# Weights of attention loaded and split by quarters inside the attention block, with scores and column sums moved around the fourth projection

## The chip, the cores and the metric

The kernel runs on one core of a Trainium2 chip. The metric is the device time of one execution in microseconds (us), and the time before is the median of three runs. A profiled execution gives the trace. TensorE is called PE there, VectorE DVE, ScalarE ACT, GpSimd POOL and SyncE SP; SPq, ACTq and PEq are the engines' sequencers, and SPq's DMA_DIRECT2D is the issue of a transfer.

## The reference, cut to what matters

Three layers follow one another, each with a residual and a LayerNorm: causal attention (scores are multiplied with a lower triangular mask, not set to minus infinity, before the softmax), a routed layer that picks one of four contexts by token, and a gated feed-forward layer with 2:4 sparsity. The change lies in the attention and in what comes ahead of it.

```python
B, T, D, HEADS = 4, 512, 512, 16
q = (x @ Wq).reshape(B, T, H, Dh); k = (x @ Wk)...; v = (x @ Wv)...
scores = jnp.einsum('bthd,bshd->bhts', q, k) * tril
attn = softmax(scores / T ** 0.5)
out = jnp.einsum('bhts,bshd->bthd', attn, v).reshape(B, T, H * Dh) @ Wo
x = layernorm(x + out)
```

## The kernel before

All of it is computed in float32 accuracy with halves: each operand is a high part (`hi`, rounded by a ScalarE copy to float32r) and a low part (`lo`, the raw value minus the high one, on VectorE), and a product is three matmuls per block of 128 rows of the contraction (hi hi, hi lo, lo hi; `matmul3`, lines 31 to 43). With D = 512 there are KT = 4 such blocks, so a product of 128 x 512 is 12 matmuls.

`prepare` (lines 1066 to 1102) is a block of its own ahead of attention. SyncE issues one load of 1 MB for each of wq, wk, wv and wo and one for x_t of batch 0 (x transposed). ScalarE copies each whole matrix to its high half and VectorE subtracts for the low half; GpSimd builds the identity that transposes need. All engines meet at the block's end, and only then does `attention` (line 46) begin.

Attention's block has a program for each engine, ordered by hand and tied by semaphores. Ahead of the loop for batch 0, ScalarE and VectorE split x_t by quarters (lines 542 and 676). TensorE then alternates for g = 0 to 3 between `project(0, g)` (even g is a q, odd g a k projection; g // 2 = m names the group of four heads; line 366) and `v_product(g)` (line 421), with the routing's counts behind g = 1. Projections all go to one PSUM bank, `PJ`. `split_proj` cuts q and k to halves (ScalarE line 517, VectorE line 640). `v_split` cuts v in three: high (ScalarE, line 547), the rest (VectorE, line 684), its bf16 half (ScalarE, line 550) and what then remains (VectorE, line 689, for batch 0; GpSimd's `v_last`, line 264, for the other batches). VectorE also makes the routing's indices in pieces between the v blocks (`route.chain`, lines 931 to 990).

SyncE's `stack_up(b, g)` (line 319) writes both halves of a projection to DRAM (lines 324 and 326), waits until they are there, and loads them again with another layout, in four transfers of 256 KB (line 332). These stacks (`big_lo` in the rows) are what the scores read. The stack g = 0 and 1 serves heads 0 to 3 (m = 0), g = 2 and 3 the next four. `G_AHEAD` is 4: four projections are made ahead of the loop.

Behind the v products come `v_sum(0, 0..2)` (nine matmuls, line 434), the column sums of v for the parts of the sequence above the diagonal; VectorE adds them up in `v_above` (lines 697 and 700). Then come the scores of units 0 to 2 (line 390), then the loop `batch(0)`. A unit is one of 48 per batch: one head and one or two blocks of rows, so that 12 units share a stack (UPM = 12). Step u of the loop does the transposes of unit u (line 401), the scores of unit u + 3, a piece of a later projection, and the values of unit u - 2 (line 417). VectorE's maxima (line 651) run two units ahead, ScalarE's exponentials (line 528) one ahead of `hi` (line 538). At u = 0 TensorE waits for all three column sums, since banks 5 and 6 hold them. SyncE loads x_t of the next batch behind the first four stacks (line 340). GpSimd adds up the parts of each head (`sum_parts`, lines 204 to 207) once ScalarE has copied them out.

## Time and profile before

| what | value |
|---|---|
| time, median of 3 runs | 1152.39 us (1150.78 to 1152.79) |
| the profiled execution | 1151.63 us, span 1149.8 us |
| TensorE busy | 1047.3 us, 91% of the span |
| VectorE, ScalarE, GpSimd busy | 751.2, 479.7, 281.9 us |
| attention of the four batches | about 22 to 465 us of the span |
| routed layer and feed-forward | from about 465 us on |

How to read it: the span is the time from the first to the last instruction of the one execution that was traced, and the shares of busy time are means over stages that have different limits. A row of the timeline names the start and duration in us, the engine, the line of the kernel, the operation, what it writes and reads, and in brackets the engine's idle time before it with what ended it. A row of the windows gives a stretch, its length, the busy time of each engine with its instructions, TensorE's mean granted clock, the busy share of the DMA engines and what they moved.

### The profile page before, as it was taken

Reading aid. Unit: us, or ns where it says so; the run is one execution under the profiler, and the core shown is the slowest. Engines: PE = TensorE matmul, PEld = TensorE weight load, DVE = VectorE, ACT = ScalarE, POOL = GpSimd, SP = SyncE. Lnnn points to the kernel's source line nnn. Section 1 sums busy time; section 2 is a strip of 40 time slices with the busy share of each in tenths; the row PEclk is TensorE's granted clock in tenths of the full one; section 3 lists DMA queues with packets and bytes.
Section 4 is the critical chain, followed back from the end, with each engine's and each line's share of the span. In section 5 each row is a group of like instructions: output and inputs, shape, how many; then the busy total and the mean of one; then the engine's idle time right before and its main releaser. Section 6 shows DMA issues by size and latency. Waiting matters only on the chain.

```text
span 1149.8 us, 18016 instructions
## 1 busy us (share of the span) xinstructions
PE 1047.3 (91%) x6022; PEld 846.0 (74%) x6023; DVE 751.2 (65%) x1764; ACT 479.7 (42%) x882; POOL 281.9 (25%) x482
## 2 busy tenths in 40 slices
PE   2898998998899976699999999999999999999994
PEld 1576766776676765488788888888888888888873
DVE  4689778868876886356664845665565545664666
ACT  4278658846864894122333322221231222222113
POOL 1036545723744462022220002300000000000222
PEclk9999999999999998799999999999999999999997
DMA  5776726735671670122444102310010101100001
GB/s 184 195 190 180 196 93 166 202 93 169 180 191 49 158 248 19 64 80 78 157 154 166 37 1 24 51 37 1 1 56 17 36 0 36 37 1 1 38 37 73
DMA packets 54016, 106.18 MB, mean 92 GB/s; under 512 B 6064, under 2 KB 6064, under 8 KB 53936
## 3 DMA queue, kind: packets, MB, share of 16 engines
q1 hardware_dynamic: 49056, 90.99, 28.5%
q0 software_dynamic: 4880, 14.18, 3.3%
q8 instruction: 44, 0.72, 0.3%
q14 instruction: 36, 0.29, 0.1%
HBM read 72.11 MB, written 30.94 MB: 90 GB/s over the span
## 4 chain that ended last, share of the span: by engine, by line
PE 56%; DVE 2%; ACT 0%; issue 0%; DMA 0%; POOLq 0%; POOL 0%; ACTq 0%; DVEq 0%
PE f_bank L42 54%; PE f_bank L1396 1%; PE f_bank L1404 1%; PE f_bank L1446 1%; DVE rows_kept L1743 0%; DVE ln_stats L810 0%; DMA rows<-sorted_dram 0%; DVE hs_lo L1731 0%; DVE xt_lo L1626 0%; DVE ln_mv L812 0%; ACT L823 0%; POOLq L1190 0%; ACT xt_hi L1512 0%; DVE h L1721 0%; ACT hs_hi L1573 0%
## 5 line engine op out<-in xcount | busy, mean ns | idle before, releaser
L1682 DVE TENSOR_TENSOR h<-f_bank,fsg 128x512 f32<-128x512 f32 x64 | 44.2, 691 | 181.6 <-PE f_bank L42 181.4
L1550 ACT ACTIVATE fsg<-f_bank 128x512 f32<-128x512 f32 x64 | 38.3, 599 | 293.8 <-PE f_bank L42 293.6
L401 PE MATMUL bank<-ident,probs 128*128 128x128 f32 x640 | 109.4, 286 | 33.5 <-DVE pt_lo L671 18.7
L528 ACT ACTIVATE probs<-bank,nmax 128x384 f32<-128x384 f32 (+3 forms) x256 | 129.8, 539 | 17.8 <-DVE nmax L662 16.3
L651 DVE CUSTOM_DVE_ANT_0 bank<-bank,mask 128x384 f32<-128x384 f32 (+3 forms) x256 | 123.1, 503 | 21.1 <-PE bank L390 20.8
L671 DVE TENSOR_TENSOR pt_lo<-bank,pt_hi 128x512 f16<-128x512 f32 (+1 forms) x192 | 114.7, 597 | 16.0 <-ACT pt_hi L538 15.8
L841 POOL TENSOR_SCALAR ln_var<-ln_mv 128x1 f32<-128x1 f32 x43 | 10.0, 233 | 466.7 <-DVE ln_mv L812 466.7
L42 PE MATMUL bank<-x_hi,w_qk 128*128 128x512 f32 x256 | 103.5, 412 | 22.8 <-DVE x_lo L676 22.4
L538 ACT ACTIVATE pt_hi<-bank 128x512 f16<-128x512 f32 (+1 forms) x192 | 103.0, 536 | 33.3 <-PE bank L401 32.6
L42 PE MATMUL f_bank<-wd_hi,hs_hi 128*128 128x512 f32 x256 | 100.4, 392 | 3.2 <-DVE rows_kept L1743 3.2
L401 PEld LDWEIGHTS bank<-ident,probs 128*128 128x128 f32 x640 | 67.2, 141 | 45.0 <-ACT probs L528 23.7
L42 PE MATMUL f_bank<-wd_hi,hs_lo 128*128 128x512 f32 x256 | 100.2, 391 | 0.0
L42 PE MATMUL f_bank<-wd_lo,hs_hi 128*128 128x512 f32 x256 | 100.1, 391 | 0.0
L42 PE MATMUL f_bank<-big_hi,wg_hi 128*128 128x512 f32 x240 | 93.8, 391 | 0.0
L42 PE MATMUL f_bank<-big_hi,wu_lo 128*128 128x512 f32 x240 | 93.5, 389 | 0.0
L42 PE MATMUL f_bank<-big_hi,wg_lo 128*128 128x512 f32 x240 | 93.4, 389 | 0.0
L42 PE MATMUL f_bank<-big_lo,wg_hi 128*128 128x512 f32 x240 | 93.4, 389 | 0.0
L42 PE MATMUL f_bank<-big_hi,wu_hi 128*128 128x512 f32 x240 | 93.4, 389 | 0.0
L42 PE MATMUL f_bank<-big_lo,wu_hi 128*128 128x512 f32 x240 | 93.4, 389 | 0.0
L390 PE MATMUL bank<-big_lo 128*128 128x384 f32 (+3 forms) x256 | 83.7, 373 | 0.0
L417 PEld LDWEIGHTS bank<-v,pt_hi 128*128 128x128 f16 x640 | 49.4, 97 | 39.0 <-issue 28.8
L417 PE MATMUL bank<-v,pt_hi 128*128 128x97 bf16 x640 | 74.7, 210 | 2.1 <-DVE pt_lo L671 1.9
(230 smaller groups left out, 2446.4 us busy)
## 6 DMA issues: line engine op xcount, KB each, us to landing
big_lo<-q_hi_dram SPq DMA_DIRECT2D x32, 256.0 KB, 4.4
big_lo<-q_lo_dram SPq DMA_DIRECT2D x32, 256.0 KB, 4.9
big_lo<-k_hi_dram SPq DMA_DIRECT2D x32, 256.0 KB, 3.7
big_lo<-k_lo_dram SPq DMA_DIRECT2D x32, 256.0 KB, 5.3
rows<-sorted_dram SPq DMA_DIRECT2D x19, 256.0 KB, 2.7
x_raw<-x_t SPq DMA_DIRECT2D x4, 1024.0 KB, 6.6
q_hi_dram<-q_hi SPq DMA_DIRECT2D x16, 256.0 KB, 2.5
q_lo_dram<-q_lo SPq DMA_DIRECT2D x16, 256.0 KB, 2.4
```

Of the source, the lines that this page charges most:

```text
L42: ins = pe.matmul(out, a(k, i), b(k, j), start=(n == 0), stop=(n == len(chain) - 1))
L390: ins = pe.matmul(S[u % SR][:, at:at + cols(r)], stack[0][m % 2][:, h, r * P:(r + 1) * P], stack[1][m % 2][:, h, 0:cols(r)], start=True, s ...
L401: ins = pe.transpose(TP[u % TR][:, j * P:(j + 1) * P], probs[u % RP][:, j * P:(j + 1) * P], ident[:, :])
L417: ins = pe.matmul(out[:, at:ONE + 1], p, v3[:, j, c, at:ONE + 1], start=(n == 0), stop=(n == len(chain) - 1))
L528: ins = act.activation(probs[u % RP][:, at:at + cols(r)], S[u % SR][:, at:at + cols(r)], ACT.Exp, bias=nmax[:, r, c:c + 1])
L538: act.activation(pt_hi[u % RP][:, 0:n], TP[u % TR][:, 0:n], ACT.Copy).then_inc(s_hi, 1)
L651: dve.tensor_tensor_reduce(out=S[u % SR][:, at:at + cols(r)], in0=S[u % SR][:, at:at + cols(r)], in1=mask[:, T - cols(r):T], scale=1.0, sc ...
L671: dve.tensor_tensor(pt_lo[u % RP][:, 0:n], TP[u % TR][:, 0:n], pt_hi[u % RP][:, 0:n], ALU.subtract).then_inc(s_lo, 1)
L1396: ins = pe.transpose(XB[q % 2][:, k * P:(k + 1) * P], rows[q][:, k * P:(k + 1) * P], ident[:, :])
L1404: ins = pe.transpose(EG[i][:, k * P:(k + 1) * P], gu[i][:, k * P:(k + 1) * P], ident[:, :])
L1550: act.activation(fsg[v % 2][:, :], GB[v % 2][:, :], ACT.Silu).then_inc(s_sg, 1)
L1682: dve.tensor_tensor(h[r % 2][:, j, :], UB[v % 2][:, :], fsg[v % 2][:, :], ALU.mult).then_inc(s_h, 1)
```

## The change

The block `prepare` is gone, and its work moves into the engine programs of `attention`. No buffers of their own hold the raw weights any more: wq lands in `probs`, wk in `v_tail` and one `v_rest`, wv in `o_raw`, wo in `z`, all of them idle at that time. SyncE issues 16 transfers of 256 KB for the weights and 4 for x_t, in the order x and wq in turn, wk, wv, the tokens, wo. ScalarE and VectorE split by quarters; the first wait is for each x and wq pair, those of the other matrices are for all four quarters. wo's low halves are subtracted by GpSimd, which also takes over the last part of v for batch 0; its clearing of `z[0]` moves behind them.

TensorE's order becomes: the projections g = 0 and 1, each block as its halves come in; the four v products; the projection g = 2; the scores of units 0 to 2; the projection g = 3; the column sums; the loop. g = 1 and 2 go to bank 4 instead of `PJ`. The cuts of g = 3 and `v_above` move into step u = 0 of the loop on ScalarE and VectorE, and TensorE waits for one column sum at u = 0 and for all of them at u = 2. The diff, cut to its core:

```diff
@@ -104,6 +104,17 @@
...
+        w_raw = [[probs[k][:, :] for k in range(KT)],
+                 [v_tail[:, k, :] for k in range(KT - 1)] + [v_rest[1][:, :]],
+                 [o_raw[:, k, :, :].rearrange("p h d -> p (h d)") for k in range(KT)],
+                 [z[k][:, :] for k in range(KT)]]
+        s_first = [sem(f"s_first{k}") for k in range(KT)]
+        s_w = [sem(f"s_w{i}") for i in range(1, len(w_dram))]
+        s_wh, s_wl = sem("s_wh"), sem("s_wl")
+        s_woh, s_wol = sem("s_woh"), sem("s_wol")
+        s_id = sem("s_id")
...
@@ -173,6 +184,10 @@
...
+        def proj_bank(b, g):
+            return bank[4] if b == 0 and g in (1, 2) else PJ
...
@@ -251,6 +266,7 @@
...
         X_HEAD = 7
+        NCONST = 6 + NB
...
@@ -266,7 +282,10 @@
...
             pool.sem_inc(s_os[1], PRIMED)
-            pool.memset(z[0][:, :], 0.0).then_inc(s_const, 1)
+            pool.memset(ident[:, :], 0.0).then_inc(s_id, 1)
+            pool.wait_ge(s_id, 1)
+            pool.affine_select(out=ident[:, :], in_=ident[:, :], compare_op=ALU.not_equal, fill=1.0, base=0,
+                               pattern=[[-1, P]], channel_multiplier=1).then_inc(s_id, 1)
...
@@ -275,10 +294,22 @@
...
                 pool.memset(n_up[:, r, :], float((NB - 1 - r) * P)).then_inc(s_const, 1)
-            pool.wait_ge(s_const, 5 + NB)
+            pool.wait_ge(s_const, 4 + NB)
...
+            for j in range(NB // 2):
+                v_last(0, j)
+            for k in range(KT):
+                pool.wait_ge(s_woh, k + 1)
+                pool.tensor_tensor(wl[3][:, k, :], w_raw[3][k], wh[3][:, k, :].bitcast(F32),
+                                   ALU.subtract).then_inc(s_wol, 1)
+            for j in range(NB // 2, NB):
+                v_last(0, j)
+            pool.wait_ge(s_wol, KT)
+            pool.memset(z[0][:, :], 0.0).then_inc(s_const, 1)
+            pool.wait_ge(s_const, NCONST)
...
@@ -312,8 +343,6 @@
...
-        NCONST = 6 + NB
...
@@ -354,7 +383,15 @@
...
+            for k in range(KT):
+                sp.dma_start(x_turned[:, k, :], x_t[0][:, k, :]).then_inc(s_first[k], 16)
+                sp.dma_start(w_raw[0][k], w_dram[0][:, k, :]).then_inc(s_first[k], 16)
+            for i in range(1, len(w_dram) - 1):
+                for k in range(KT):
+                    sp.dma_start(w_raw[i][k], w_dram[i][:, k, :]).then_inc(s_w[i - 1], 16)
             route.load(sp)
+            for k in range(KT):
+                sp.dma_start(w_raw[-1][k], w_dram[-1][:, k, :]).then_inc(s_w[-1], 16)
...
@@ -365,14 +402,18 @@
...
                 m, side = g // 2 % NM, g % 2
-                if first == 0:
-                    pe.wait_ge(s_pjl, b * 2 * NM + g)
-                if g < 2 * NM:
+                if first == 0 and (b > 0 or g > 1):
+                    pe.wait_ge(s_pjl, b * 2 * NM + g - (b == 0 and g == G_AHEAD - 1))
+                if b == 0 and g < 2:
+                    pe.wait_ge(s_xl, last // 3)
+                    pe.wait_ge(s_wl, g * KT + last // 3)
+                elif g < 2 * NM:
...
                     pe.wait_ge(s_xl, (b + 1) * KT + (last + 2) // 3)
-                ins = matmul3(pe, PJ[:, :], lambda k, i: (wh, wl)[i][side][:, k, m * P:(m + 1) * P],
+                ins = matmul3(pe, proj_bank(b, g)[:, :], lambda k, i: (wh, wl)[i][side][:, k, m * P:(m + 1) * P],
...
@@ -418,15 +459,22 @@
...
-            def v_product(j):
-                matmul3(pe, VB[j][:, :], lambda k, i: x_hl[i][:, k, j * P:(j + 1) * P],
-                        lambda k, i: (wh, wl)[i][2][:, k, :], KT).then_inc(s_vp, 1)
+            def v_product(j, fresh=False):
+                for first in range(0, 3 * KT, 3):
+                    if fresh:
+                        pe.wait_ge(s_wl, 2 * KT + first // 3 + 1)
+                    ins = matmul3(pe, VB[j][:, :], lambda k, i: x_hl[i][:, k, j * P:(j + 1) * P],
+                                  lambda k, i: (wh, wl)[i][2][:, k, :], KT, first, first + 3)
+                ins.then_inc(s_vp, 1)
...
                     pe.wait_ge(s_v2, (b + 1) * NB)
+                    if b == 0:
+                        pe.wait_ge(s_const, NCONST - 1)
...
@@ -453,6 +501,9 @@
...
                 pe.wait_ge(s_otl, b * NB + r + 1)
+                if b == 0 and r == 0:
+                    pe.wait_ge(s_wol, KT)
...
@@ -463,7 +514,10 @@
...
-                        pe.wait_ge(s_sfe, (b + 1) * (NB - 1))
+                        pe.wait_ge(s_sfe, (b + 1) * (NB - 1) if b > 0 else 1)
+                    if u == 2 and b == 0:
+                        pe.wait_ge(s_sfe, NB - 1)
...
@@ -494,16 +548,22 @@
...
-            for g in range(G_AHEAD):
-                project(0, g, 0, 3 * KT)
-                v_product(g)
-                if g == 1:
-                    pe.wait_ge(s_const, NCONST)
+            for g in range(2):
+                for first in range(0, 3 * KT, 3):
+                    project(0, g, first, first + 3)
+            for j in range(NB):
+                v_product(j, j == 0)
+                if j == 1:
+                    pe.wait_ge(s_const, NCONST - 1)
                     route.count(pe, ones_bf[:, :], counts[0], counts[1])
+            project(0, 2, 0, 3 * KT)
+            pe.wait_ge(s_vr, AHEAD_S)
+            for u in range(AHEAD_S):
+                scores(0, u)
+            project(0, 3, 0, 3 * KT)
...
                 v_sum(0, n)
-            for u in range(AHEAD_S):
-                scores(0, u)
+            pe.wait_ge(s_id, 2)
...
@@ -514,7 +574,7 @@
...
                 act.wait_ge(s_dw, b * 2 * NM * 32 + max(g - 1, 0) * 32)
-                act.activation(qk_hl[side][0][:, :], PJ[:, :], ACT.Copy,
+                act.activation(qk_hl[side][0][:, :], proj_bank(b, g)[:, :], ACT.Copy,
...
@@ -538,7 +598,10 @@
...
             def x_split(b, k):
-                act.wait_ge(s_xraw, (b + 1) * 16)
+                if b == 0:
+                    act.wait_ge(s_first[k], 32)
+                else:
+                    act.wait_ge(s_xraw, b * 16)
...
@@ -584,6 +647,8 @@
...
                         exps(b, u)
+                    if b == 0 and u == 0:
+                        split_proj(0, G_AHEAD - 1)
...
@@ -622,11 +687,25 @@
...
+            def weight_hi(i, k, done):
+                if i > 0:
+                    act.wait_ge(s_w[i - 1], KT * 16)
+                act.activation(wh[i][:, k, :], w_raw[i][k], ACT.Copy).then_inc(done, 1)
...
                 x_split(0, k)
-            for g in range(G_AHEAD):
-                split_proj(0, g)
-                v_split(0, (g,))
+                weight_hi(0, k, s_wh)
+            for i in (1, 2):
+                for k in range(KT):
+                    weight_hi(i, k, s_wh)
+                split_proj(0, i - 1)
+            for j in range(NB):
+                v_split(0, (j,))
+                if j == 0:
+                    for k in range(KT):
+                        weight_hi(3, k, s_woh)
+            split_proj(0, 2)
...
@@ -637,7 +716,7 @@
...
                 dve.wait_ge(s_pjh, b * 2 * NM + g + 1)
-                dve.scalar_tensor_tensor(out=qk_hl[side][1][:, :], in0=PJ[:, :],
+                dve.scalar_tensor_tensor(out=qk_hl[side][1][:, :], in0=proj_bank(b, g)[:, :],
...
@@ -684,10 +763,6 @@
...
                                       ALU.subtract).then_inc(s_vr, 1)
-                for j in blocks if b == 0 else ():
-                    dve.wait_ge(s_v1, b * NB + j + 1)
-                    dve.tensor_tensor(v3[:, j, :, V2:V2 + HD], v_rest[j % 2][:, :].rearrange("p (h d) -> p h d", d=HD),
-                                      v3[:, j, :, V1:V1 + HD], ALU.subtract).then_inc(s_v2, 1)
...
@@ -737,6 +812,10 @@
...
                         split_proj(b, split_at[u])
+                    if b == 0 and u == 0:
+                        split_proj(0, G_AHEAD - 1)
+                        for n in range(NB - 1):
+                            v_above(0, n)
...
@@ -763,18 +842,27 @@
...
+            def weight_lo(i, k):
+                dve.wait_ge(s_wh, i * KT + k + 1)
+                dve.tensor_tensor(wl[i][:, k, :], w_raw[i][k], wh[i][:, k, :].bitcast(F32),
+                                  ALU.subtract).then_inc(s_wl, 1)
...
                 x_split(0, k)
+                weight_lo(0, k)
+            for i in (1, 2):
+                for k in range(KT):
+                    weight_lo(i, k)
+                split_proj(0, i - 1)
             routing = route.chain(dve, counts[0], counts[1])
-            for g in range(G_AHEAD):
-                split_proj(0, g)
-                v_split(0, (g,))
+            for j in range(NB):
+                v_split(0, (j,))
...
-            dve.wait_ge(s_const, NCONST)
-            for n in range(NB - 1):
-                v_above(0, n)
+            split_proj(0, 2)
+            dve.wait_ge(s_const, NCONST - 1)
...
@@ prepare, lines 1066 to 1102 @@
-def prepare(nc, w_dram, w_split, ident, x_src, x_turned, s_xraw, D):
...
```

## Rows read from the trace of the kernel before

**Rows 1.** Busy us by stage: length, PE, PEld, DVE, ACT, POOL, clock, DMA, GB/s.

```profile
0.00:18.80 18.80, 0.00 (x0) 0.01 (x1) 9.17 (x4) 8.92 (x5) 0.68 (x6) 1.00 0.76 279
...
22.40:27.10 4.70, 4.67 (x13) 3.77 (x14) 0.00 (x0) 0.00 (x0) 0.03 (x1) 1.00 0.00 0
...
27.10:47.40 20.30, 19.88 (x87) 15.52 (x85) 12.15 (x41) 6.08 (x10) 0.00 (x0) 1.00 0.69 182
```

**Rows 2.** Timeline of the start: SyncE's last load, ScalarE's splits of wq, wk, wv.

```profile
3.20 2.32 SPq L1083 DMA_DIRECT2D x_raw<-x_t  x1
...
6.22 1.91 ACT L1096 ACTIVATE w_qk<-w_raw 128x2048 fp32r<-128x2048 f32 x1 [4.13 <-DMA w_raw<-wq]
...
9.12 1.91 ACT L1096 ACTIVATE w_qk<-w_raw 128x2048 fp32r<-128x2048 f32 x1 [0.99 <-DMA w_raw<-wk]
...
11.82 1.91 ACT L1096 ACTIVATE big_hi<-w_raw 128x2048 fp32r<-128x2048 f32 x1 [0.79 <-DMA w_raw<-wv]
```

**Rows 3.** DMA issues of the first 8 us: the load of x_t, KB, us to landing.

```profile
x_raw<-x_t SPq DMA_DIRECT2D x1, 1024.0 KB, 14.0
```

**Rows 4.** The timeline from the column sums into the loop, TensorE and VectorE.

```profile
50.19 3.73 PE L434 MATMUL bank<-v,ones_bf 128*128 128x512 bf16 x9 [2.81 <-DVE v L689]
...
53.55 0.99 PE L390 MATMUL bank<-big_lo 128*128 128x384 f32 x4
...
56.64 0.88 PE L401 MATMUL bank<-ident,probs 128*128 128x128 f32 x4 [2.09 <-ACT probs L528]
...
58.14 0.57 DVE L651 CUSTOM_DVE_ANT_0 bank<-bank,mask 128x384 f32<-128x384 f32 x1 [0.88 <-PE bank L390]
...
71.05 0.48 PE L390 MATMUL bank<-big_lo 128*128 128x384 f32 x2
```

**Rows 5.** The busy time of a stretch in batch 0's loop, in columns as above.

```profile
90.00:100.00 10.00, 7.38 (x85) 5.99 (x82) 9.93 (x40) 10.00 (x25) 5.74 (x10) 1.00 0.83 210
```

**Rows 6.** SyncE's timeline, and the landing of all stack loads from 28 to 60 us.

```profile
39.74 0.43 SPq L332 DMA_DIRECT2D big_lo<-k_lo_dram  x1
...
40.94 0.34 SPq L326 DMA_DIRECT2D q_lo_dram<-q_lo  x1
...
46.93 0.32 SPq L332 DMA_DIRECT2D big_lo<-q_hi_dram  x1
...
55.22 0.79 SPq L332 DMA_DIRECT2D big_lo<-k_hi_dram  x2
...
57.08 0.40 SPq L340 DMA_DIRECT2D x_raw<-x_t  x1
...
66.90 0.34 SPq L324 DMA_DIRECT2D q_hi_dram<-q_hi  x1
...
DMA to landing us min/median/max: 3.0/4.6/5.7
```

**Rows 7.** The timeline's splits of x_t by quarters on ScalarE and VectorE.

```profile
19.03 2.19 ACT L542 ACTIVATE x_hi<-x_raw 128x512 fp32r<-128x512 f32 x4 [2.60 <-PEq L1072]
...
19.69 2.59 DVE L676 TENSOR_TENSOR x_lo<-x_raw,x_hi 128x512 fp32r<-128x512 f32 x4 [0.94 <-ACT x_hi L542]
```

**Rows 8.** The chain that ended last: one product of 12 matmuls in the routed layer.

```profile
498.59 2.80 PE f_bank L42 x12
```

**Rows 9.** The timeline: VectorE's one-hots ahead of the counts, and a cut of k.

```profile
32.62 0.17 DVE L946 CAST tok_f<-tok_sb 128x16 f32<-128x16 int32 x1
...
32.75 0.60 ACT L517 ACTIVATE k_hi<-bank 128x512 fp32r<-128x512 f32 x1 [0.78 <-PE bank L42]
...
35.25 0.69 DVE L640 SCALAR_TENSOR_TENSOR k_lo<-bank,k_hi 128x512 fp32r<-128x512 f32 x1
```

**Rows 10.** Two lines of GpSimd: duration ns min/median/max, first and last start.

```profile
L264 POOL TENSOR_TENSOR v<-v_rest,v x12: 1122/1138/1150, 138.8 to 352.2; 128x512 bf16<-128x512 f32 x12
...
L259 POOL TENSOR_TENSOR x_lo<-x_raw,x_hi x12: 1269/1284/1302, 94.6 to 306.1; 128x512 fp32r<-128x512 f32 x12
```

**Rows 11.** TensorE's stretches of 1 us: length, busy us, granted clock, DMA share, GB/s.

```profile
51.00:52.00 1.00, 1.00 (x4) 0.50 1.04 203
```

More of the change, by code:

```diff
@@ L43, in matmul3, with attention @@
     return ins
-def attention(nc, w_split, stacks, ident, idx_all, x_t, x_raw, s_xraw, x_rows,
+def attention(nc, w_dram, w_split, stacks, ident, idx_all, x_t, x_raw, s_xraw, x_rows,
               sorted_rows, route, context, scratch, B, T, D):
@@ L1855, in build @@
             x_raw = actx.enter_context(nc.sbuf_tensor("x_raw", [P, KT * T], F32))
-            x_turned = x_raw[:, :].rearrange("p (k t) -> p k t", k=KT)
             w_vo = big[0][:, 0:4 * KT * D].rearrange("p (i k n) -> p i k n", i=4, k=KT)
@@ L1859, in build @@
             x_t = x_t.rearrange("b (k p) t -> b p k t", p=P)
-            prepare(nc, [w.rearrange("(k p) n -> p k n", p=P) for w in (wq, wk, wv, wo)], w_split, ident,
-                    x_t[0], x_turned, s_xraw, D)
-            attention(nc, w_split, big[1], ident, idx_all, x_t, x_raw, s_xraw,
+            w_dram = [w.rearrange("(k p) n -> p k n", p=P) for w in (wq, wk, wv, wo)]
+            attention(nc, w_dram, w_split, big[1], ident, idx_all, x_t, x_raw, s_xraw,
                       x.rearrange("b (r p) d -> b p r d", p=P), sorted_rows,
```

30 lines of the change are left out of this document (removed).

## The prediction, made before the changed kernel ran

> **What bounds the kernel now.** I read the busy time by stage first. Up to 18.8 us TensorE does nothing: the weights are loaded and split whole [rows 1]. It then works from 22.4 us on, 19.88 of the 20.3 us from 27.1 to 47.4 [rows 1], and has gaps again before the loop of batch 0 [rows 4]. Next comes the order of events at the start. The five loads of 1 MB are issued by 5.5 us [rows 2] and land one after the other: ScalarE waits for wq until 6.2 us, for wk until 9.1, for wv until 11.8 [rows 2], and x_t lands 14.0 us after its issue at 3.2 [rows 2, 3], so at 17.2. One more MB takes some 2.7 us. x_t, which everything needs, comes last, and attention starts only behind wo's splits. That head of about 22.4 us lies wholly on the path: nothing after it is tied to absolute time. The loop starts with the transposes at 56.64 us; VectorE takes up its work on unit 3 at 58.14 us [rows 4]. In the loop VectorE and ScalarE are all but full (9.93 and 10.00 of 10 us) [rows 5]. So whoever brings the loop's start forward by n us gains n us, whatever the 91% of TensorE on the page say, as long as the loop finds its stacks and buffers in time. The task is to compute the new start.
>
> **New loads.** The order becomes x and wq in pairs of quarters, then wk, wv, the tokens, wo. The bytes and the rows of 2 KB (512 floats) are the same, so I keep 2.7 us per MB and the landing times of the sequence in which the matrices arrived: the first pair (0.5 MB) at 4.8 us, the next ones 1.4 us apart (6.2, 7.6, 9.1), wk at 11.8, wv at 14.5, wo at 17.2 [rows 2, 3]. SyncE issues 21 transfers at 0.43 us each (the issue at 39.74) [rows 6] and a little between them, say 0.47, and is through at about 10.5 us, before it has anything else to do.
>
> **Splits.** A quarter costs ScalarE about 0.56 us (2.19 us for four) and VectorE 0.65 (2.6 us for four) [rows 7]; whole matrices cost 1.91 us on ScalarE [rows 2], so cutting costs some 0.3 us a matrix, hidden behind the loads. Pair 3 lands at 9.1; its x and w highs are done at 10.25, its lows at 11.05. TensorE starts at about 6.6 us and ends the first q projection at 11.7 to 12.3. Although wk comes in quarters, its splits wait for all four: ScalarE 11.8 to 14.05, VectorE to 15.0, TensorE's k projection to 15.7, fed by quarters. ScalarE cuts q only behind wk's highs (14.7), VectorE q's low at 15.7. wv: highs 14.7 to 16.9, k's high at 17.5, wv's lows to 18.4, k's low 19.1. The first v product ends at 19.1.
>
> **TensorE's path from there.** A product of 12 matmuls is 2.8 us at full rate [rows 8], 4.7 in the cold start [rows 1]. v product 1 ends at 21.9. Then the counts wait for the one-hots, which VectorE makes behind the first v cut: 20.5 plus 2.6 us (32.62 to 35.22 before) [rows 9] is 23.1, a stall of 1.2 us. v products 2 and 3 end at 29.1, the projection of g=2 at 31.9. The other costs here are nil, by their covers: wo's highs (2.2 us of ScalarE between the cuts of v blocks 0 and 1) lie beside the v products, and delay v's cut 1 by 1.4 us, which is made good by block 2; without that cover they would cost 2.2. wo's lows and the last v halves go to GpSimd: 4 x 1.28 + 4 x 1.14 = 9.7 us [rows 10]. Two v halves are done at 25.8, wo's lows at 31.0, the other two at 33.3 us, and the column sums want them only after the fourth projection, at about 37.4. Queued behind these on GpSimd are the clearing of z[0] and the first sums of parts, which come only some 9 us into the loop. VectorE is rid of four subtractions of 0.69 us.
>
> **The stacks, SyncE's chain.** This is what I take to be last. q's high and low writes are issued at 14.7 and 15.8 us, but queue behind wo, which lands at 17.2; before, the writes issued at 40.94 behind a stack's loads were seen done at 46.93, about 1.6 us after these loads had landed (39.74 + 5.7) [rows 6]. So q's loads start at 18.8. From the first load of a q stack to the first load of the k stack it was 46.93 to 55.22, 8.3 us, with k's halves ready, as they are here: 27.1. The last of four loads is issued three issues of 0.43 us later and lands within 3.0 to 5.7 us [rows 6]: 31.4 to 34.1; nothing queues behind it here, and I take 33.6. So the first scores start at 33.6, against TensorE free at 31.9: moving the scores ahead of projection 3 makes the stack's wait show, but also covers the projection's own stack.
>
> **From the scores to the loop.** Scores 1.0 us, projection 3 2.8 us (37.4), its high on ScalarE 0.6 and low on VectorE 0.7 behind the first maxima (38.8), v_above(0) 0.7 like the low [rows 4, 9]: the transposes start at 39.5. TensorE's three column sums (2.1 us warm; 3.73 in the row) [rows 4] run beside this. VectorE's sums 1 and 2 follow and unit 3's maxima come at 41.0, where they came at 58.14. Gain: 56.64 - 39.5 = 17.1 by the one, 17.1 by the other. Two corrections by the clock. Before the scores TensorE idles 1.7 us. After an idle of 2.8 us, and again after 2.1 us, the trace has some 3 us at a granted clock of 0.5, i.e. 1.2 GHz [rows 4, 11]; the column sums took 1.6 us more than at full rate. I charge 1.7 us (bounds 0 and 3.4, the second if the counts' stall does it too). In return the new loop starts with TensorE just busy for 6 us, where the old one lost its first 3 to 4 us at 0.5 clock; VectorE was idle 0.9 of them, as far as I see it from its rows; I credit 0.9 (bounds 0 and 1.5). Sum: 17.1 - 1.7 + 0.9 = 16.3 us. The profiled execution took 1151.63 us (span 1149.8), which gives 1135.3; the median before is 1152.39, 0.8 above it, and gives 1136.
>
> **After the loop has started.** Stack g=2 is loaded from 35.2 us (1.6 behind the k stack's landing), g=3 8.3 later, from 43.5, landed at about 50: 10.5 us into the loop. It is wanted at unit 12, issued 14.4 us into the loop (71.05 to 56.64) [rows 4]: 4 us of slack. The x_t load of batch 1 follows and lands near 54; before, it came at 0.4 us into the loop [rows 6], now at 6. g=4's writes, ready some 10 us into the loop (66.90) [rows 6], queue behind it: q's loads at 16 us into the loop, k's at 24, landed at 30.5, wanted at unit 24, which I put at twice unit 12's time and a little, 31 to 33. That costs nothing, but with 1 to 2 us of slack; if the cover is gone, TensorE waits there for as long as it is short.
>
> **A rule that speaks against it.** The Trainium skill, "DMA: Bandwidth & Descriptors", section "Bandwidth", says to batch a DMA to 1 MiB or more, since at 64 KB it measured 138 GB/s and at 1 MB 341. An estimate half way between (240 GB/s) would move the 5.2 MB in 21.8 us instead of about 14, and would take 8 us off the gain. Against that, no row of this trace has 256 KB loads of whole rows into 128 partitions queued back to back; rival C has the price by rows.
>
> **The rivals.**
> A, the forecast: the k stack ends last, gain 14.5 to 18: 1134.4 to 1137.9. Chance 0.54.
> B: the stack is in time and TensorE's path is the last: scores at 31.9, and no idle before them, so no cold stretch. Gain 17.1 + 1.7 + 0.9 = 19.7: 1132.7. For it: the loads landed in as little as 3.0 us. Against: 8.3 us per stack. Chance 0.13.
> C: the loads or the clock are worse. Quarters at the pace of the stack loads (1 MB within 1.3 + 5.7 us of the first issue, less some 1.7 us until data move, makes 200 GB/s) put wo's end at about 28 instead of 17.2 us and leave a gain of 5 to 6 (1146 to 1147); chance 0.05. Two cold stretches instead of one, a TensorE that stays at 1.2 GHz while it is fed by quarters, or a stack that comes late at unit 12 or 24, cost 1.7 to 4 us more, gain 12 to 14.5: 1138 to 1140; chance 0.21. If it never reached full rate, eight products at 4.7 to 5.1 us put the loop at about 53, still faster.
> D, slower: the transfers of one queue don't overlap, so that each quarter costs its issue to landing. wv is then through after 16 quarters. Break-even is where 17 us are lost, i.e. wv at 31.5: 1.9 us a quarter. At 2.5 us, wv lands at 41, the loop starts at about 66, and the time is 1161 or more. For it: loads of 256 KB show 3.0 to 5.7 us [rows 6]. Against: a group of four lands some 7 us after its first issue (1.3 + 5.7), not 4 x 4.6. Chance 0.03.
> E, same: the gain is given back, because a step of batch 0 hangs on GpSimd or a stack after all (it would have to be 16 us late). Chance 0.02. The last 0.02 go to what I don't see.
> That the quarters of wk and wv are waited for together, so that they bring nothing over whole loads, is in the forecast.
>
> **Range and chances.** From B's 1132.7, less 1 for a kinder clock, to C's second kind at 1140 plus 1: 1131.5 to 1141; this leaves out about 0.12. A difference of 0.2% (2.3 us) is about what can be told from no change. Faster by more than that 0.94, within it 0.03, slower 0.03.
>
> **What would show it.** The first matmul at 6 to 7 us; x and wq pairs 1.4 us apart; the first stack loads at 18 to 20 and the k stack's at 26 to 28 us; first scores at 33 to 34 with a wait for a DMA ahead of them; transposes at 38 to 42; then stretches of the same length as before. Scores ahead of 32 us would speak for B; a pair pitch of over 2 us for C or D; a short wait of TensorE for a stack at unit 12 or 24 for C, a long one, or one of ScalarE for GpSimd's sums, for E. The prediction is wrong if the loop's start moves by other than 14 to 18 us, or if the shift isn't carried to the end one for one.

## The result, and the profile after

The changed kernel takes 1136.74 us (median of 4 executions, 1136.54 to 1141.51) against 1152.49 us before, a gain of 15.75 us by the medians. The ratio, which compares the means, is 0.9876 with a 95% interval of 0.9849 to 0.9904, i.e. 14.3 us. Two repeats gave 1139.35 us (ratio 0.9889, 0.9851 to 0.9928) and 1141.12 us (0.9881, 0.9859 to 0.9903). The 14 executions lie in two groups, seven from 1135.7 to 1137.9 and seven from 1140.8 to 1142.3 us; why is told below. Their median, 1139.35, is 13.2 us under the 1152.5 of the kernel before in the same three sets of runs. This is the better figure of the gain.

The profiled execution of the change is one of the upper group (1141.51 us, span 1139.8). Where the result of the first four leaves that open, I use the repeat `e0_repeat` (1137.91 us, span 1136.2). First the timeline of the change at the start, ScalarE, VectorE and TensorE:

```profile
4.16 0.63 ACT L605 ACTIVATE x_hi<-x_raw 128x512 fp32r<-128x512 f32 x1 [2.07 <-DMA probs<-wq]
...
6.26 0.77 PE L42 MATMUL bank<-x_hi,w_qk 128*128 128x512 f32 x1 [6.26 <-DVE w_qk L848]
...
7.24 0.63 ACT L605 ACTIVATE x_hi<-x_raw 128x512 fp32r<-128x512 f32 x1 [1.93 <-DMA probs<-wq]
...
9.82 0.63 ACT L605 ACTIVATE x_hi<-x_raw 128x512 fp32r<-128x512 f32 x1 [0.19 <-DMA probs<-wq]
...
12.41 1.67 ACT L694 ACTIVATE w_qk<-v_tail 128x512 fp32r<-128x512 f32 x3 [1.43 <-DMA v_rest<-wk]
```

The first matmul comes at 6.26 us instead of 22.43. The pairs are there at 4.2, 7.2 and 9.8 us (the third was ready while ScalarE was still at the second), wk at 12.4. Next, from the counts to the loop; these rows answer to [rows 4] and [rows 9]:

```profile
24.83 0.19 PE L1016 MATMUL bank<-onehot_bf,before 128*128 128x64 bf16 x1 [2.15 <-DVE run L1042]
...
33.54 0.87 PE L431 MATMUL bank<-big_lo 128*128 128x384 f32 x4
...
37.81 2.21 PE L482 MATMUL bank<-v,ones_bf 128*128 128x512 bf16 x9 [0.64 <-POOL v L280]
...
42.95 0.63 PE L442 MATMUL bank<-ident,probs 128*128 128x128 f32 x4 [2.93 <-DVE v_tail L772]
...
44.38 0.56 DVE L730 CUSTOM_DVE_ANT_0 bank<-bank,mask 128x384 f32<-128x384 f32 x1
```

The scores come at 33.54, with no idle time before them. The loop starts at 42.95 (56.64 before), after 2.93 us in which TensorE waited for VectorE's `v_above`; unit 3's maxima come at 44.38 (58.14). SyncE's timeline, which answers to [rows 6]:

```profile
19.05 0.32 SPq L361 DMA_DIRECT2D big_lo<-q_hi_dram  x1
...
26.91 0.79 SPq L361 DMA_DIRECT2D big_lo<-k_hi_dram  x2
...
148.63 0.40 SPq L369 DMA_DIRECT2D x_raw<-x_t  x1
```

What VectorE did between 21 and 38 us is the surprise. VectorE's and GpSimd's timeline in the change:

```profile
21.64 1.52 DVE L1038 TENSOR_SCALAR ge<-tok_f 128x16 f32<-128x16 f32 x3
...
21.99 1.15 POOL L280 TENSOR_TENSOR v<-v_rest,v 128x512 bf16<-128x512 f32 x1 [18.11 <-ACT v L613]
...
25.80 2.83 DVE L1050 TENSOR_TENSOR run<-run 128x64 f32<-128x64 f32 x4
...
27.26 5.04 POOL L306 TENSOR_TENSOR big_hi<-z,big_hi 128x512 fp32r<-128x512 f32 x4
...
28.66 1.21 DVE L1053 TENSOR_TENSOR rank<-run,total 128x64 f32<-128x64 f32 x1
...
30.17 0.69 DVE L763 TENSOR_TENSOR v_rest<-bank,v 128x512 f32<-128x512 f32 x1
...
31.10 1.22 DVE L1059 TENSOR_SCALAR n_tiles<-n_pad 128x4 int32<-128x4 int32 x1
...
32.35 1.06 DVE L1061 TENSOR_SCALAR n_rows<-n_tiles 128x4 int32<-128x4 int32 x1
...
36.61 1.14 POOL L280 TENSOR_TENSOR v<-v_rest,v 128x512 bf16<-128x512 f32 x1 [3.22 <-ACT v L613]
...
37.07 1.18 DVE L1077 CAST tile_expert<-expert_f 128x19 int32<-128x19 f32 x1
...
37.70 0.52 POOL L311 MEMSET z<- 128x512 f32 x1
...
38.37 0.68 DVE L719 SCALAR_TENSOR_TENSOR q_lo<-bank,q_hi 128x512 fp32r<-128x512 f32 x1
```

The same steps before, from the groups by line (busy us and mean ns of one):

```profile
L962 DVE TENSOR_TENSOR run<-run 128x64 f32<-128x64 f32 x4 | 0.9, 225 | 0.1
...
L965 DVE TENSOR_TENSOR rank<-run,total 128x64 f32<-128x64 f32 x1 | 0.2, 224 | 0.0
...
L971 DVE TENSOR_SCALAR n_tiles<-n_pad 128x4 int32<-128x4 int32 x1 | 0.2, 170 | 0.0
```

A step of 0.17 or 0.22 us takes 1.06 to 1.22 us when it meets a subtraction of GpSimd, and ends with it or just behind. The last one, L1077, ends at 38.25 us, not with the subtraction (37.75) but just behind the clearing of `z[0]` that follows it (38.22). Line by line against before this adds 0.9 (L1038) + 1.8 (L1050) + 1.0 (L1053) + 0.1 (L1058) + 1.0 (L1059) + 0.9 (L1061) + 1.0 (L1077), some 6.8 us, on VectorE's way to the first maxima. A cut that reads a PSUM bank (L763 at 30.17) keeps its 0.69 us in the midst of GpSimd's four.

### The profile page after: what moved, and what is told of

The parts are those of the page before. It is cut to its first block, busy times and chain, and to the rows that moved or that the text cites. A ratio compares the mean times of both kernels' runs of the same rounds, so it can differ in the third digit from the quotient of the medians.

```text
span 1139.8 us, 18047 instructions
## 1 busy us (share of the span) xinstructions
PE 1050.1 (92%) x6022; PEld 847.2 (74%) x6023; DVE 751.8 (66%) x1768; ACT 480.5 (42%) x894; POOL 291.1 (26%) x490
## 4 chain that ended last, share of the span: by engine, by line
PE 56%; DVE 2%; DMA 1%; ACT 0%; issue 0%; POOLq 0%; POOL 0%; ACTq 0%; SPq 0%; DVEq 0%
PE f_bank L42 54%; PE f_bank L1453 1%; PE f_bank L1445 1%; PE f_bank L1495 1%; DVE rows_kept L1792 0%; DVE ln_stats L898 0%; DMA fw_raw<-gate 0%; DMA rows<-sorted_dram 0%; DVE hs_lo L1780 0%; DVE gu L1696 0%; ACT L911 0%; DVE ln_mv L900 0%; POOLq L1239 0%; DVE h L1770 0%; DVE ln_shift L918 0%
## 5 line engine op out<-in xcount | busy, mean ns | idle before, releaser
L442 PE MATMUL bank<-ident,probs 128*128 128x128 f32 x640 | 109.9, 287 | 34.9 <-DVE pt_lo L750 19.1
L588 ACT ACTIVATE probs<-bank,nmax 128x384 f32<-128x384 f32 (+3 forms) x256 | 130.0, 540 | 14.9 <-DVE nmax L741 13.5
L750 DVE TENSOR_TENSOR pt_lo<-bank,pt_hi 128x512 f16<-128x512 f32 (+1 forms) x192 | 114.6, 597 | 15.8 <-ACT pt_hi L598 15.4
```

The source lines that it names most:

```text
L442: ins = pe.transpose(TP[u % TR][:, j * P:(j + 1) * P], probs[u % RP][:, j * P:(j + 1) * P], ident[:, :])
L588: ins = act.activation(probs[u % RP][:, at:at + cols(r)], S[u % SR][:, at:at + cols(r)], ACT.Exp, bias=nmax[:, r, c:c + 1])
L750: dve.tensor_tensor(pt_lo[u % RP][:, 0:n], TP[u % TR][:, 0:n], pt_hi[u % RP][:, 0:n], ALU.subtract).then_inc(s_lo, 1)
```

## The experiments

All start from the changed kernel. The loop's start is the first row of TensorE's transposes of batch 0; it is read from one profile each and carries the clock of the head alone, while the time of a whole execution also carries the stretches at half clock shown next. The loads differ by up to 1 us between profiles, and TensorE's start on the routing's counts (24.83 us in the change) carries that difference. From there to the loop's start it is 18.1 us in the change, in both repeats, in e6 and in e10.

**e0_repeat and e7_repeat2: the change again, unaltered.**

> The changed kernel once more, unaltered. The profiled execution of the change took 1141.5 us against 1136.6 in its other executions, so it is no good base for comparisons of a microsecond. Its start should repeat: transposes of the loop at 42 to 43.5 us, vector engine's small routing steps stretched. If the 5 us were a matter of chance in later stages (a load of the feed-forward weights was waited for in the chain, and batch 2 lost 1.6 us), this profile shows a span near 1135 and stretches between landmarks as in the kernel before. If they belong to the change, the profile shows them again and the time is 1141.

> The changed kernel unaltered, to be compared with the three above on one chip: loop's start at 42.6 to 43 us, 1136.5 to 1139.5, in steps of 1.6 us by how many stretches at half clock an execution has.

Measured: 1139.35 and 1141.12 us (the second above the 1136.5 to 1139.5 expected); the loops start at 42.57 and 43.11 us. The head repeats within 0.5 us, the whole does not, so the 5 us between executions are not the head's. The loop's start in e0_repeat:

```profile
42.57 0.63 PE L442 MATMUL bank<-ident,probs 128*128 128x128 f32 x4 [2.93 <-DVE v_tail L772]
```

TensorE's stretches of 3.8 and 4 us (length, busy, granted clock, DMA share, GB/s), first in the profiled execution of the change, then in e0_repeat:

```profile
43.00:47.00 4.00, 3.05 (x15) 0.60 1.08 228
...
47.00:50.80 3.80, 3.80 (x20) 0.52 0.52 174
```

```profile
43.00:47.00 4.00, 2.55 (x24) 1.00 1.06 213
47.00:50.80 3.80, 3.80 (x36) 1.00 0.56 188
```

Both had waited 2.93 us for VectorE. One then ran at 1.2 GHz for some 6.5 of its next 7.8 us, the other at 2.4 GHz. The same event by SyncE's load of x_t for batch 2, in the kernel before, e0_repeat and e7_repeat2 (148.63 in the change):

```profile
160.47 0.40 SPq L340 DMA_DIRECT2D x_raw<-x_t  x1
```

```profile
146.17 0.40 SPq L369 DMA_DIRECT2D x_raw<-x_t  x1
```

```profile
148.80 0.40 SPq L369 DMA_DIRECT2D x_raw<-x_t  x1
```

The change is 11.8 us ahead of before there (13.7 at its loop's start), e0_repeat 14.3 (14.1 at its loop's start). From the loop's start to this load it is 105.7 us in the change and in e7_repeat2, which started at half clock too (0.63 and 0.50 in the two stretches), and 103.6 in e0_repeat: the cold start costs 2.1 us. Each of the three has one more short stretch at half clock in the batches (at 150 us in e0_repeat, at 256 in the other two), so these don't set them apart. The routed layer does: its first two products, 12 matmuls each, take 5.21 and 4.61 us in the change, 4.44 and 3.05 in e0_repeat (granted clock in the second 0.64 and 1.00), and e7_repeat2 is like the change. The second one, in the chain that ended last, in the change and then in e0_repeat:

```profile
466.97 4.61 PE f_bank L42 x12
```

```profile
464.75 3.05 PE f_bank L42 x12
```

Loop's start 0.4, cold start 2.1, routed layer 2.3 us make 4.8; some 1.2 us are given back, most of it ahead of the routed layer, and the spans differ by 3.6.

**e1_thin_wo: GpSimd's subtractions for wo all but removed.**

```diff
-                pool.tensor_tensor(wl[3][:, k, :], w_raw[3][k], wh[3][:, k, :].bitcast(F32),
+                pool.tensor_tensor(wl[3][:, k, 0:8], w_raw[3][k][:, 0:8], wh[3][:, k, 0:8].bitcast(F32),
```

The kernel leaves out the other 504 columns of wo's low halves; four copies of the mask on GpSimd, from 3.94 to 7.14 us, fill them.

> GpSimd's four subtractions for wo's low halves take 8 of 512 columns; the rest of the low half is filled from another tile earlier, so the output isn't the reference's. Theory 1: in the profile of the change VectorE's small steps of the routing on SBUF operands took 1.0 to 2.8 us instead of 0.2 to 1.0 whenever GpSimd subtracted, some 6.7 us in all, because the two engines get in each other's way at SBUF. Then without the four long subtractions about 4 us of this are gone, VectorE cuts v block 3 and q of g=2 that much earlier, and the loop starts at 39.5 to 41 instead of 42.95 us: 1134 to 1135.5. Theory 2: these steps are slow for another reason (fetching of instructions, the tokens): they stay as slow, and the time is 1136.7. Theory 3: the stack of k, not VectorE, sets the loop's start: the steps get quick, but the time stays at 1136.7.

Measured: 1135.38 us (ratio 0.9862, 0.982 to 0.9903). The loop starts at 40.41 us, 2.2 earlier than in e0_repeat, and 2.7 earlier counted from the counts (15.4 against 18.1 us), since the head is later here: the copies meet two of VectorE's first splits, which take 0.96 and 1.09 us instead of 0.69, and the first matmul comes at 6.82 instead of 6.26. VectorE's and TensorE's timeline:

```profile
29.59 0.17 DVE L1063 TENSOR_SCALAR n_tiles<-n_pad 128x4 int32<-128x4 int32 x1
29.79 0.17 DVE L1065 TENSOR_SCALAR n_rows<-n_tiles 128x4 int32<-128x4 int32 x1
...
40.41 0.63 PE L446 MATMUL bank<-ident,probs 128*128 128x128 f32 x4 [0.85 <-issue]
```

The steps that no longer meet a long subtraction are back at 0.17 us. VectorE's excess falls from 6.8 to some 3.7 us; four steps still meet the four subtractions of v. Theory 1 holds, theory 2 (slow for another reason) falls, and so does theory 3, as the loop's start moved with VectorE. At 33.87 us the scores waited 0.25 us for the stack, so the stack and TensorE's own work are level there.

**e2_order: scores and column sums back in the old order.** The cuts of g=3 and `v_above` go back ahead of the loop with them.

```diff
-            pe.wait_ge(s_vr, AHEAD_S)
-            for u in range(AHEAD_S):
-                scores(0, u)
             project(0, 3, 0, 3 * KT)
             for n in range(NB - 1):
                 v_sum(0, n)
+            for u in range(AHEAD_S):
+                scores(0, u)
```

> The order of scores and column sums undone: projections 2 and 3, column sums, then the scores of units 0 to 2, with the cuts of g=3 and the sums on VectorE ahead of the loop, as before; loads and splits stay as changed. By the rows of the change the column sums can't start before 37.8 us (last v part on GpSimd), the scores would come at 40.1, and the loop about 3.1 us later, 43.2 to 44.2 us instead of 42.95: 1137 to 1138.5, so the reordering is worth 0.3 to 2 us. If the reordering were what brought the gain, the time would be above 1142.

Measured: 1139.46 us (0.9888, 0.9852 to 0.9924), above the 1137 to 1138.5 expected; loop's start 43.74 against 42.57 to 43.11:

```profile
43.74 0.63 PE L442 MATMUL bank<-ident,probs 128*128 128x128 f32 x4 [3.18 <-ACT probs L587]
```

The next maxima, unit 3's, came at 44.8 against 44.0 to 44.5. By these the reordering is worth 0.3 to 0.8 us in the changed kernel; counted from the counts, 0.9 at the loop's start and 0.5 at the maxima. Nearly all of the gain is the loads' and splits'.

**e3_warm: TensorE kept busy ahead of the loop.**

```diff
+            pe.wait_ge(s_pjl, 3)
+            for n in range(12):
+                pe.matmul(bank[4][:, :], ones_bf[:, :], v3[:, 0, :, V0:V0 + HD], start=True, stop=True)
             pe.wait_ge(s_id, 2)
```

> Twelve idle matmuls (2.8 us, result unused, into bank 4) fill TensorE's wait ahead of the loop. Theory: that wait of 2.9 us takes the granted clock to 0.5 for the first microseconds of the loop, and of the 13.8 us that the loop's start had gained only 11.9 were left 15 maxima later. With TensorE kept busy the loop runs at full clock and 1 to 1.9 us come back: 1135 to 1135.7. Rival: VectorE sets the pace of the loop anyway: no change, 1136.7.

Measured: 1139.72 us (0.9889, 0.9853 to 0.9924). Its profiled execution has full clock from 38 to 57 us, but so has e0_repeat without the idle matmuls, and the loop's start (42.38) is 0.2 us away. The executions (1138.57, 1138.88, 1140.56, 1141.17) show no gain; none came near the 1135 to 1135.7 expected. One profile can't tell whether the idle matmuls prevent a cold start; this stays open.

**e4_better and e5_better_old_order: VectorE relieved.** The one-hots move to a wait between the first pairs, the counts ahead of the v products, wo's highs and lows ahead of v; e5 has the old order of scores and sums on top. The core of the edit (the one-hots' steps on VectorE and GpSimd's new order left out):

```diff
+                if k == 0:
+                    route.load(sp)
...
+            pe.wait_ge(s_const, NCONST - 1)
+            route.count(pe, ones_bf[:, :], counts[0], counts[1])
             for j in range(NB):
                 v_product(j, j == 0)
...
+            for k in range(KT):
+                weight_hi(3, k, s_woh)
             for j in range(NB):
                 v_split(0, (j,))
```

> The changed kernel with VectorE kept clear of GpSimd: tokens loaded behind the first pair, the one-hots made in VectorE's wait between the first two pairs, the counts ahead of the v products, wo's highs in ScalarE's wait ahead of v block 0, wo's lows first on GpSimd and the last v parts behind them. Theory 1 (the small routing steps are held up by GpSimd's subtractions, and the counts by the one-hots): TensorE's wait of 2.15 us at the counts goes, VectorE's steps between the v cuts fit into their gaps of 2.1 us each, the scores wait for the k stack till 33.5 to 34, and the loop starts at 39.4 to 40 us against 42.6 to 42.9 in the change: some 3 us less, 1134 to 1135.5 (or 1.6 more for each stretch at half clock that falls in). Theory 2 (the k stack is what bounds the change): the loop's start moves by under 1 us. Rival 3: wo's lows now collide with wv's lows on VectorE at 16 to 19 us, each of which is held up by up to 1.2 us, and the first v product and with it all is later by 2 to 3 us: no gain.

> The run before with the order of scores and column sums undone: projection 3, column sums, then the scores. If the k stack bounds the scores (33.5 to 34 us), projection 3 and the sums fit ahead of it (they would end near 36.5), the scores come at 36.5 and the loop 3.1 us later at 39.5 to 40: the reordering is worth 0 to 0.5 us there. If the stack is ready earlier than that, the reordering is worth more, 1 to 2 us.

Measured: e4 1135.97 us (0.9856, 0.9833 to 0.9879), e5 1136.32 us (0.985, 0.983 to 0.987). In e4 the wait at the counts is gone. VectorE isn't rid of the collisions: some 4.0 us of excess are left (6.8 before the edit). But it has its one-hots done by 8.5 us and cuts v block 3 at 32.42 instead of 35.18 us, and the k stack is what TensorE now waits for. Its timeline and granted clock:

```profile
34.06 1.51 PE L430 MATMUL bank<-big_lo 128*128 128x384 f32 x4 [2.84 <-DMA big_lo<-k_lo_dram]
...
39.09 2.21 PE L481 MATMUL bank<-v,ones_bf 128*128 128x512 bf16 x9
41.30 0.63 PE L441 MATMUL bank<-ident,probs 128*128 128x128 f32 x4
```

```profile
34.00:37.40 3.40, 3.34 (x9) 0.50 0.42 151
```

After an idle of 2.84 us TensorE ran 3.4 us at 1.2 GHz: the scores took 1.51 us instead of 0.87, and projection 3 ended at 39.1, 5.0 us behind the scores' start, where it is 3.5 in e8: 1.5 us lost. So the loop starts at 41.30, 1.3 to 1.9 us behind what was expected, and e5, which has no such wait, starts its loop at 40.66. My sum for e4 had the stack right (33.5 to 34) and had left out the cold stretch behind it. The times don't differ beyond their spread, and e4's is a little above the 1134 to 1135.5 expected: the reordering brings nothing while it makes TensorE wait for the stack. Rival 3 falls too: wv's four lows take 2.49 us, as in the change.

**e6_pairs_whole: no work before all of x and wq is there.**

```diff
-                    act.wait_ge(s_first[k], 32)
+                    for kk in range(KT if k == 0 else 0):
+                        act.wait_ge(s_first[kk], 32)
```

> The changed kernel, but ScalarE starts to split x and wq only when all four pairs have landed, as if both had been loaded whole. By the rows of the change the last pair lands at 9.8 us; the first low of wq is then done at about 11.8, the first matmul at 11.9 instead of 6.3, the q projection ends at 16.5 instead of 13.4, k's at 19.3 to 20 instead of 16.9, so TensorE is 2.5 to 3 us later; ScalarE and VectorE are behind by as much, as their 8 splits each can't begin early. Theory: the quarters of the pairs are worth what VectorE loses, 2 to 3.5 us at the loop's start (45 to 46): 1139 to 1142. Rival: the order of loading alone (x and wq first) brings all of the gain, as later stages wait anyway: under 1 us.

Measured: 1143.82 us (0.9925, 0.9906 to 0.9944), the loop starts at 47.62 us, 4.5 to 5.1 us late, more than the 2 to 3.5 expected. The timelines of ScalarE and TensorE have what I had missed:

```profile
9.94 1.28 ACT L606 ACT_TABLE_LOAD   x1 [9.94 <-DMA probs<-wq]
11.23 0.63 ACT L606 ACTIVATE x_hi<-x_raw 128x512 fp32r<-128x512 f32 x1
...
13.34 0.76 PE L42 MATMUL bank<-x_hi,w_qk 128*128 128x512 f32 x1 [13.34 <-DVE w_qk L849]
...
47.62 0.63 PE L442 MATMUL bank<-ident,probs 128*128 128x128 f32 x4 [2.59 <-DVE v_tail L773]
```

The load of ScalarE's table, which otherwise runs at 0.81 us beside the first transfers, fell behind the waits and added 1.28 us. Less these 1.28 us the quarters of the first pairs are worth some 3.2 to 3.8 us. The rival (the order of loading alone brings it all) falls. One thing more: behind its wait at the counts TensorE ran at 1.2 GHz here from 29.5 to 32.7 us, and its scores came 9.9 us behind the counts instead of 8.7 to 9.0. The loop's start did not move by it (18.1 us behind the counts, as in the change), which again puts VectorE last.

**e8_better_early_k, e9_old_order_early_k, e10_early_k: the stack's chain shortened.** SyncE writes k's halves ahead of q's loads, under a semaphore of their own. The same edit goes into e4, e5 and the changed kernel:

```diff
+            for g, done in ((0, s_dw), (1, s_dk)):
+                sp.wait_ge(s_pjh, g + 1)
+                sp.dma_start(scratch[g][0], qk_hl[g][0][:, :].bitcast(F32)).then_inc(done, 16)
+                sp.wait_ge(s_pjl, g + 1)
+                sp.dma_start(scratch[g][1], qk_hl[g][1][:, :].bitcast(F32)).then_inc(done, 16)
+            wait_apart(sp, s_passed_sp, [(s_dw, 32)])
+            stack_loads(0)
+            wait_apart(sp, s_passed_sp, [(s_dk, 32)])
+            stack_loads(1)
```

> e4_better with one change on SyncE: k's two writes to DRAM are issued ahead of q's four loads (19.3 us), so that k's four loads follow q's at once instead of 8.1 us after the first of them. Theory: in e4 the k stack is what ends last (TensorE waited 2.84 us for it, then ran 3.4 us at half clock). Now q's loads start at about 19.7, k's at 21.5, and the 2 MB are in by 31 to 32.5 us instead of 34.1; TensorE waits for under 1 us, no stretch at half clock, and the loop starts at 38.8 to 39.5 us instead of 41.3: 1133 to 1134.5. Rival: VectorE, which cuts v block 3 at 32.4 and q of g=2 at 34.3 us, is now as late as the stack: scores at 32, loop's start at 39.5 to 40.5, 1134 to 1135.5. If the stack was not the bound in e4: 1136.

> The same with the old order of scores and column sums (e5 with k's writes early). There the scores come behind the column sums, which wait for the last part of v on GpSimd (35.4 us), and not for the stack: the loop's start stays at 40.7 us and the time at 1136. The reordering of the change would then be worth 1.2 to 1.9 us here, where it was worth nothing in e4 against e5.

> The changed kernel itself with k's writes ahead of q's loads and nothing else. Theory: its loop's start is set by VectorE (routing steps held up by GpSimd, v block 3 cut at 35.2, q of g=2 at 38.4) and the stack comes no later than TensorE's own work (33.4 to 33.9 us): no change at the loop's start, 42.6 to 43.1 us, 1136 to 1141 by the clock. Rival, the forecast's step: the k stack is last in the change: the loop would start 1.5 to 2 us earlier.

Measured: e8 1135.37 us (0.985, 0.9821 to 0.9878), e9 1137.39 us (0.9865, 0.9842 to 0.9889), e10 1141.69 us (0.9894, 0.9868 to 0.9921); each is 0.7 to 1.4 us above what was expected. The timelines of SyncE and TensorE in e8:

```profile
19.89 0.35 SPq L398 DMA_DIRECT2D big_lo<-q_hi_dram  x1
...
21.80 0.83 SPq L398 DMA_DIRECT2D big_lo<-k_hi_dram  x2
```

```profile
31.98 0.87 PE L448 MATMUL bank<-big_lo 128*128 128x384 f32 x4 [0.71 <-DMA big_lo<-k_lo_dram]
...
39.02 0.63 PE L459 MATMUL bank<-ident,probs 128*128 128x128 f32 x4 [1.35 <-issue]
```

k's loads start 1.9 us after q's, no longer 8.1 as in e4, and the scores 2.1 us earlier, without a cold stretch; the loop starts at 39.02, 2.3 us earlier. e9's loop starts at 41.05, as e5's did at 40.66: the old order waits for the v sums, not for the stack. Between e8 and e9 lie 2.0 us, of which 0.9 are the head's, as e9 came to its counts at 18.0 us and e8 at 17.0: the reordering is worth 1.1 us here. e10's loop starts no earlier than the change's:

```profile
43.43 0.63 PE L460 MATMUL bank<-ident,probs 128*128 128x128 f32 x4 [2.93 <-DVE v_tail L790]
```

That is 18.1 us behind its counts, the same as in the change, though k's loads were issued at 22.0 instead of 26.9 us: in the change the stack is not what ends last. e8 has the lowest start of all. Its time is the lowest too, but its interval overlaps those of e4 and e5, whose executions spread by several us.

## Why the prediction was right, and where it was not

The time forecast was 1136.0, measured 1136.74. That it came this close is luck: the median of all 14 executions is 1139.35, six of them and the second repeat (1141.12) lie above the range's end of 1141, and the gain by the 14, 13.2 us, is what the forecast had given to rival C's second kind (12 to 14.5), not to A (14.5 to 18). The gain at the loop's start was forecast at 17.1 us and is 13.5 to 14.1. The prediction's own signs (14 to 18 us at the loop's start, carried to the end one for one) hold in e0_repeat alone, with 14.1 us at the loop's start and 13.6 in the span. In the profiled change it is 13.7 and 10.0, in e7_repeat2 13.5 and 10.2. Step by step:

- **The head falls away and the rest moves with it**: right, but for the clock. From the loop's start to the load of x_t for batch 2 e0_repeat keeps 14.1 to 14.3 us, and the chain's last long piece of matmuls starts at 645.44 us before and at 631.98 there, 13.5 us earlier. In the change it starts at 635.55, 9.9 us earlier: half-clock stretches, at the loop's start and in the routed layer, took the rest.
- **Loads**: first matmul 6.26 (said 6.6). The last pair was there at 9.8 (9.1) and wk at 12.4 (11.8), so the quarters are 0.6 to 0.7 us late in all. Rivals C (200 GB/s) and D fall: from 6.2 to 13.4 us the queue moved 379 GB/s. So does, for 256 KB queued back to back, the estimate of 8 us lost that I had made from the Trainium skill's rule on DMAs of 1 MiB ("DMA: Bandwidth & Descriptors", section "Bandwidth").
- **TensorE's path**: q projection to 13.4 (11.7 to 12.3), v product 0 to 19.7 (19.1), stall at the counts 2.15 (1.2), free for the scores at 33.5 (31.9). Of these 1.6 us, 0.9 are the one-hots held up by GpSimd, the rest the later loads.
- **The stack**: q's loads at 19.05 (18.8), k's at 26.91 (27.1), scores at 33.54 (33.6). Each term holds; but what I took to be last was only level with TensorE, which waited 0.3 and 0.2 us for it in the repeats and not at all in the change. e10 shows that it isn't the bound, e4 and e8 that it becomes one once VectorE is relieved.
- **The step that failed** is "The other costs here are nil, by their covers", about wo's lows and the v halves on GpSimd. I had only worked out that GpSimd is in time for its readers (the column sums came at 37.81 after 0.64 us of waiting for it, said 37.4) and not what its instructions do to VectorE. By the sum's own terms VectorE could have cut v block 3 at about 29.7 us (product at 29.1, ScalarE 0.6) and q of g=2 at 32.5 (31.9 and 0.6); it did so at 35.18 and 38.37. e1 shows the cause. Mostly through it the loop starts at 42.6 to 43.1 instead of 39.5; e1, with half of the collisions gone, starts at 40.41. The later loads have a part in the rest (0.7 us).
- **The clock**: I charged one cold stretch ahead of the scores. There was none, since TensorE had no wait there; the 2.9 us wait came later, ahead of the loop, and made the loop start at 1.2 GHz in the change and e7_repeat2 (2.1 us) and not in e0_repeat. The credit of 0.9 us against the cold start of before [rows 11] is too large: from the loop's start to the load of x_t for batch 2 it was 103.8 us before and 103.6 in e0_repeat, 0.2 less. The first four executions happened to hold three of the quick group; with the cold stretch that was charged and did not come, that covered most of what VectorE lost. The number is right for a part of the wrong reason.
- **Stacks in the loop**: k's loads for g=3 were issued at 49.01 us (said 43.5), 6.1 us into the loop, and the gain did not shrink at unit 12 or 24. The slack, said to be thin, was enough: TensorE waits for no stack in the loop.

The Trainium skill, "SBUF — State Buffer", section "SBUF: two separate sides", says that VectorE and GpSimd share one pair of ports under an exclusive lock: an operation of VectorE in a two-port mode or with two SBUF inputs and one of GpSimd (for the two inputs, one that reads SBUF) shut each other out, until the one that has the lock ends. The trace agrees: tensor_tensor, tensor_scalar and casts on SBUF operands went from 0.17 to 0.22 us to as much as 1.22, close to the length of GpSimd's 1.14 to 1.29 us, while the cut with a PSUM input stayed at 0.69. Read against the change, this rule would have put an estimate of up to 9.7 us, the length of the eight subtractions by [rows 10], on VectorE, where the forecast had nothing; 6.8 us came of it.

The trace before had a sign of it that I overlooked. In the loop of batch 0 two steps of one shape, both with two SBUF inputs, take 0.96 us beside a long subtraction of GpSimd and 0.21 without one (timeline of VectorE and GpSimd):

```profile
99.03 2.52 POOL L259 TENSOR_TENSOR x_lo<-x_raw,x_hi 128x512 fp32r<-128x512 f32 x2
...
99.42 0.96 DVE L1056 TENSOR_TENSOR at<-at,gap 128x64 f32<-128x64 f32 x1
...
101.70 0.21 DVE L1059 TENSOR_TENSOR at<-at,onehot 128x64 f32<-128x64 f32 x1
```

## What to carry to other kernels

Work moved to an idle engine isn't free because that engine is idle: before it is costed at nothing, list which of the neighbour's instructions read SBUF in the same stretch, and what each of them holds up. When a head is shortened, write down every chain that runs to the loop's start (here TensorE, VectorE, SyncE's stacks) with its time: removing one cause showed the next within 3 us, at times with a cold TensorE behind it. A reordering is worth what the new last wait allows: the same one brought 0.3 to 0.8, nothing, and 1.1 us in three neighbours of one kernel. Where the executions of one kernel spread by 6 us, a median of four can be 2 to 3 us off; a landmark in the trace, counted from an earlier one, repeated here within 0.1 us.

## What the runs showed of the hardware that was not expected

- A small VectorE step on SBUF operands waits out a GpSimd subtraction on SBUF operands: 0.17 us becomes 1.06 to 1.22 us, about one step for each GpSimd instruction (6.8 us over eight such instructions in the change, 3.7 in e1, where four of them are long). The larger splits of 128x512 with two SBUF inputs are held up as well (0.96 and 1.09 us instead of 0.69 beside GpSimd's copies, e1). A cast waited out GpSimd's clearing of `z[0]` too (1.18 us, the change); in e3_warm it ran between subtraction and clearing and took 0.72.
- Equal waits of 2.93 us of TensorE were followed by a granted clock of 1.00 in e0_repeat and e10 and of 0.50 to 0.63 over 7.8 us in the change and e7_repeat2, which cost 2.1 us by the loads of x_t. Equal waits of 2.14 to 2.15 us at the counts were followed by full clock in the change and by 3 us at half clock in e6. With further stretches at half clock, in the batches and in the routed layer, this spreads the executions of one kernel over 1135.7 to 1142.3 us. That such stretches explain both groups is read from three profiles and not shown for each execution.
- ScalarE's table load ran at 0.81 us, hidden, when its first instruction had a single wait ahead of it, and at 9.94 us, behind the data, when four stood there (e6); it takes 1.28 us.
- Eight stack loads of 256 KB queued without a wait between them were in 12.1 us after the first was issued (19.89 to 31.98, e8), where the same eight with k's writes in between took 14.9 (19.12 to 34.06, e4). In both TensorE was waiting for the last of them.
